# One TensorE tile shape throughout, and the last batch tile's top layers in pieces on two engines

## The chip, the cores and the metric

The kernel runs on one core of one Trainium2 chip. The metric is the device time of one execution in microseconds, the median of the runs. The kernel before takes 656.53 us (3 runs, 656.3 to 657.41).

## The reference

A recommendation tower for 1024 samples. 32 embedding tables give `e` (1024 x 32 x 16). A compressed interaction network of three layers of 64 maps follows, and then three dense layers:

```python
x0 = xk = e
for W in (W0, W1, W2):                      # (32,32,64), (32,64,64), (32,64,64)
    xk = relu(einsum('bmd,bhd,mhk->bkd', x0, xk, W))
    outs.append(sum(xk, axis=2))
z = concatenate(outs, axis=1)               # 1024 x 192
h = concatenate([z, dense_ctx], axis=1)     # 1024 x 208
h = maximum(h @ W_top1 + b_top1, 0)         # 512
h = maximum(h @ W_top2 + b_top2, 0)         # 256
y = h @ W_top3                              # 1
```

All of it is computed in float32.

## The kernel before, in words

The batch is cut into 8 tiles of 128 samples; a tile has two sides (A, Bs) of 64 samples, and a side two blocks of 32 samples, 512 columns (sample, d) each. Partitions hold pairs (m, h). The work is a list of 48 phases (tile, layer, side), lines 56 to 62, in which the layers of neighbouring tiles and sides are interleaved. In the steady part the order is (i, 2, A), (i+1, 0, A), (i, 2, Bs), (i+1, 0, Bs), (i+1, 1, A), (i+1, 1, Bs).

A phase is a list of steps. In each step VectorE (L692) or GpSimd (L401) multiplies the current maps by a copy of x0, 128 x 1024, into a ring (`z`, 6 places; `z_pool`, 4 places), and TensorE multiplies the product with 128 x 64 weights (L470), once per block: block 0 writes PSUM partitions 0 to 63 of the phase's accumulator, block 1 partitions 64 to 127. Two matmuls of 128 x 64 x 512, in two column groups of the array, are a step; the profile has each matmul as two records. Layers 1 and 2 have 16 steps, of which GpSimd makes 3 to 5 (line 66). Layer 0 has 4 steps, for the pairs of different embeddings, and one more product for the diagonal: ScalarE squares 32 rows (L521) and TensorE multiplies them by 32 x 64 weights (L466), from partitions 0 to 31 for side A and 32 to 63 for side Bs.

ScalarE fills the operand banks `xk` in PSUM (L535, L544, L553, L560), empties the accumulators (L571 for the next layer, L577 for the sums) and copies the sums of the layers, which VectorE reduces (L668), into the inputs of the top layers, `in12` and `in3` (L589). The top layers of tile i-1 are put into the step lists of tile i by hand (H1_AT, H2_AT, Y_AT, line 154): make_h1 (L417, L418) before step 12 of (i, 1, Bs), make_h2 (L425) before step 6 and make_y (L432) before step 13 of (i, 2, A). Each is a run of matmuls of 128 x 128 (80 x 128; 128 x 1 for y) on 128 streamed columns into one PSUM bank, `top`; ScalarE takes the results (L596, L603, L611).

GpSimd's queue carries, besides its products, the gathers of the embeddings of later tiles (L355). SP's queue stores gathered rows to DRAM (L275), loads them back as `lay`, `x0rep` and `squares` (L284, L296, L288) when their buffers are free, and, between the loads of side A and of side Bs, waits for y of tile i-2, loads the context rows (L340) and stores y (L341). ScalarE's queue loads the weights at the start.

After the last step the kernel runs 4 filler matmuls on 512 columns (L409), make_h1, 2 fillers, make_h2 and make_y for tile 7, each waiting for ScalarE's whole step before it (line 477 to 481, 649 to 654).

Of the kernel before, what the change touches and what calls it, by code (L numbers as in the profile page):

```python
# [15 lines left out]
H = 64  # L16
# [123 lines left out]
SUM_ROWS = [(layer, side) for layer in range(3) for side in range(SIDES)]  # L140
SUMS = {}
# [15 lines left out]
N_TOP_LOADS = 8  # L157


def build(nc, ids, ctx_t, tables, sel, ident, w0a, w0b, w0d, w1, w2, wt1, bt1, wt2, bt2, wt3, out):  # L160
    with ExitStack() as stack:
# [7 lines left out]
        w0d_sb = sb("w0d_sb", [SIDES * M, H])  # L169
# [13 lines left out]
        squares = sb("squares", [SIDES * M, WIDE])  # L183
# [11 lines left out]
        y_sb = sb("y_sb", [1, P])  # L195
# [32 lines left out]
        reduced = sem("reduced")  # L228
        inputs_in = sem("inputs_in")
        unit_ready = sem("unit_ready")  # L230
        unit_taken = sem("unit_taken")
        y_out = sem("y_out")

# [13 lines left out]
        def _(sp):  # L247
# [38 lines left out]
            def load_rows(i, side):  # L286

                sp.dma_start(squares[side * M:(side + 1) * M, :],  # L288
                             bass.AP(x0_rows, columns(i, side), [[PITCH, M], [1, WIDE]])).then_inc(rows_in[side], 16)
# [40 lines left out]
            for i in range(1, NT):  # L330
# [6 lines left out]
                if i > 1:  # L337
# [3 lines left out]
                    sp.dma_start(out[i - 2:i - 1, :], y_sb[:]).then_inc(y_out, 16)  # L341
# [5 lines left out]
            sp.dma_start(out[i - 2:i - 1, :], y_sb[:]).then_inc(y_out, 16)  # L347
            sp.wait_ge(unit_taken, 3 * (NT - 1) + 3)
            sp.dma_start(out[NT - 1:NT, :], y_sb[:]).then_inc(y_out, 16)
# [55 lines left out]
        def _(pe):  # L405
            def keep_busy(count, at):

                for _ in range(count):
                    pe.matmul(at[0:H, :], w1_sb[:, 0, :],  # L409
                              w1_sb[:, 0:COLS // H, :].rearrange("p t k -> p (t k)"), start=True, stop=True)  # L410

            def make_h1(i):
                pe.wait_ge(inputs_in, i + 1)
                pe.wait_ge(ctx_in, 16 * (i + 1))
                for m in range(F1 // P):
                    o = top[:, m * P:(m + 1) * P]
# [12 lines left out]
            def make_y(i):  # L429
                pe.wait_ge(unit_taken, 3 * i + 2)  # L430
                for k in range(F2 // P):
                    last = pe.matmul(top[0:1, 0:P], wt3_sb[:, k:k + 1], h2[:, k, :],  # L432
                                     start=(k == 0), stop=(k == F2 // P - 1))
                last.then_inc(unit_ready, 1)

# [7 lines left out]
            for n, (i, layer, side) in enumerate(PHASES):  # L443
# [5 lines left out]
                for k, (who, tile, _, _) in enumerate(STEPS[n]):  # L449
# [25 lines left out]


            keep_busy(4, xk[:, 0, 0:COLS])
            make_h1(NT - 1)
            keep_busy(2, xk[:, 0, 0:COLS])
            make_h2(NT - 1)  # L480
            make_y(NT - 1)

        @block.scalar
        def _(act):
# [18 lines left out]
            for side in range(SIDES):  # L503
                act.dma_start(w0d_sb[side * M:(side + 1) * M, :], w0d).then_inc(top_in, 16)
# [12 lines left out]
            def square(i, side):  # L517

                act.wait_ge(rows_in[side], 16 * (i + 1))
                of_side = squares[side * M:(side + 1) * M, :]  # L520
# [58 lines left out]
            def inputs(i, rows=range(len(SUM_ROWS))):  # L579
# [10 lines left out]
                if row == len(SUM_ROWS) - 1:  # L590
                    op.then_inc(inputs_in, 1)

# [14 lines left out]
            def take_y(i):  # L607
# [3 lines left out]
                act.activation(y_sb[:], top[0:1, 0:P], ACT.Copy).then_inc(unit_taken, 1)  # L611
# [38 lines left out]
            evacuate(taken)  # L650
            inputs(NT - 1, range(len(SUM_ROWS) - 1, len(SUM_ROWS)))
            take_h1(NT - 1)
# [96 lines left out]
```

## Time and profile before

| | us |
|---|---|
| median of 3 runs | 656.53 |
| the profiled execution, its own time | 655.24 |
| its span, first to last instruction | 653.3 |
| TensorE busy | 586.3 (90%) |
| VectorE busy | 545.9 (84%) |
| GpSimd busy | 513.9 (79%) |
| ScalarE busy | 353.2 (54%) |

TensorE's clock was granted in full (2.4 GHz) for 0.984 of the span; below it lie the start and a stretch after 222 us. Times in the rows are us from the span's start. Engines: PE is TensorE's matmuls, PEld its weight loads, DVE VectorE, ACT ScalarE, POOL GpSimd, SP the DMA-issuing engine. Matmuls are pipelined and the ends of their records are modelled, so the distance between starts tells their cost, not the duration.

### The profile page before, as it was taken

Reading aid. Unit: us, or ns where it says so; the run is one execution under the profiler, and the core shown is the slowest. Engines: PE = TensorE matmul, PEld = TensorE weight load, DVE = VectorE, ACT = ScalarE, POOL = GpSimd, SP = SyncE. Lnnn points to the kernel's source line nnn. Section 1 sums busy time; section 2 is a strip of 40 time slices with the busy share of each in tenths; the row PEclk is TensorE's granted clock in tenths of the full one; section 3 lists DMA queues with packets and bytes.
Section 4 is the critical chain, followed back from the end, with each engine's and each line's share of the span. In section 5 each row is a group of like instructions: output and inputs, shape, how many; then the busy total and the mean of one; then the engine's idle time right before and its main releaser. Section 6 shows DMA issues by size and latency. Waiting matters only on the chain.

```text
span 653.3 us, 7670 instructions
## 1 busy us (share of the span) xinstructions
PE 586.3 (90%) x2692; PEld 200.6 (31%) x2692; DVE 545.9 (84%) x345; ACT 353.2 (54%) x540; POOL 513.9 (79%) x373
## 2 busy tenths in 40 slices
PE   0027789899999799999999999999999999999998
PEld 0002223232333233332343324332333333333434
DVE  0002989899998799999999999999999998999780
ACT  0002574455756447555666666555755576666541
POOL 6777769388889888988898888888888876568650
PEclk9999799999999799999999999999999999999999
DMA  8649999950189917994499639990899249950000
GB/s 256 174 54 250 253 177 238 271 159 4 17 179 234 244 32 134 236 233 97 66 248 234 154 29 218 233 222 8 166 224 248 59 81 255 219 133 0 1 2 0
DMA packets 88438, 98.67 MB, mean 151 GB/s; under 512 B 59880, under 2 KB 66416, under 8 KB 88384
## 3 DMA queue, kind: packets, MB, share of 16 engines
q1 hardware_dynamic: 76064, 90.11, 60.4%
q0 software_dynamic: 8192, 2.11, 3.2%
q10 hardware_dynamic: 4144, 5.96, 2.8%
q8 instruction: 21, 0.34, 0.2%
q14 instruction: 17, 0.14, 0.1%
HBM read 95.01 MB, written 7.61 MB: 157 GB/s over the span
## 4 chain that ended last, share of the span: by engine, by line
PE 69%; DVE 6%; DMA 5%; ACT 5%; issue 2%; DVEq 0%; ACTq 0%
PE acc L470 61%; DVE z L692 6%; DMA x0rep<-x_rows 5%; ACT xk L560 3%; PE top L425 2%; PE acc L466 2%; PE top L417 1%; PE top L418 1%; PE xk L409 1%; ACT xk_copy L571 1%; PE top L432 1%; ACT xk L535 0%; ACT squares L521 0%; ACT xk L553 0%; DVEq L688 0%
## 5 line engine op out<-in xcount | busy, mean ns | idle before, releaser
L692 DVE TENSOR_TENSOR z<-xk,x0rep 128x2048 f32<-128x2048 f32 (+1 forms) x295 | 520.1, 1821 | 55.2 <-DMA x0rep<-x_rows 26.9
L470 PE MATMUL acc<-z,w_sb 128*64 128x512 f32 x1852 | 439.6, 605 | 20.3 <-DVE z L692 20.0
L401 POOL TENSOR_TENSOR z_pool<-x0rep,xk_copy 128x1024 f32<-128x1024 f32 x113 | 268.6, 2379 | 49.6 <-PE acc L470 32.2
L355 POOL DMA_INDIRECT emb<-tbl,idx x256 | 245.1, 957 | 68.6 <-issue 62.4
L470 PEld LDWEIGHTS acc<-z,w_sb 128*64 128x64 f32 x1852 | 128.4, 138 | 298.9 <-issue 225.3
L560 ACT ACTIVATE xk<-xk_copy 32x1024 f32<-32x1024 f32 x128 | 130.5, 1019 | 102.7 <-DVE z L692 101.4
L470 PE MATMUL acc<-z_pool,w_sb 128*64 128x512 f32 x452 | 116.4, 593 | 0.0
L571 ACT ACTIVATE xk_copy<-acc 64x512 f32<-64x512 f32 x128 | 75.5, 590 | 8.7 <-PE acc L470 7.6
L553 ACT ACTIVATE xk<-lay 128x1024 f32<-128x1024 f32 x16 | 16.4, 1028 | 78.3 <-DVE z L692 62.4
L409 PE MATMUL acc<-w_sb 128*64 128x512 f32 x24 | 12.4, 665 | 44.1 <-DMA emb<-tbl,idx 44.1
L470 PEld LDWEIGHTS acc<-z_pool,w_sb 128*64 128x64 f32 x452 | 32.1, 137 | 63.1 <-issue 60.8
L668 DVE TENSOR_REDUCE row_sums<-layer_out 128x32 f32<-128x512 f32 x48 | 32.3, 674 | 5.9 <-ACT layer_out L577 5.9
L535 ACT ACTIVATE xk<-xk_copy 128x1024 f32<-128x1024 f32 x31 | 31.7, 1022 | 7.8 <-DVE z L692 7.4
L577 ACT ACTIVATE layer_out<-acc 128x512 f32<-128x512 f32 x48 | 28.5, 594 | 8.5 <-PE acc L470 7.6
L535 ACT ACTIVATE xk<-lay 128x1024 f32<-128x1024 f32 x16 | 16.4, 1028 | 27.2 <-DMA lay<-x_rows 25.1
L660 DVE TENSOR_TENSOR w_sb<-w_sb,z 128x256 f32<-128x256 f32 x1 | 0.4, 424 | 34.5 <-DMA w_sb<-w0a_twice 34.5
L589 ACT ACTIVATE in<-row_sums 64x32 f32<-64x32 f32 x96 | 21.8, 227 | 6.7 <-DVE row_sums L668 5.7
L409 PEld LDWEIGHTS acc<-w_sb 128*64 128x64 f32 x24 | 3.6, 154 | 51.7 <-issue 51.7
L521 ACT ACTIVATE squares<-squares 32x1024 f32<-32x1024 f32 x16 | 16.8, 1050 | 4.5 <-DMA squares<-x_rows 4.3
L466 PE MATMUL acc<-squares,w0d_sb 32*64 32x512 f32 x64 | 18.1, 642 | 0.1
L425 PEld LDWEIGHTS top<-h,wt_sb 128*128 128x128 f32 x128 | 14.9, 191 | 6.5 <-issue 5.7
L535 ACT ACT_TABLE_LOAD x1 | 1.3, 1283 | 28.1 <-issue 28.1
(19 smaller groups left out, 97.6 us busy)
## 6 DMA issues: line engine op xcount, KB each, us to landing
x0rep<-x_rows SPq DMA_DIRECT2D x128, 512.0 KB, 16.0
lay<-x_rows SPq DMA_DIRECT2D x32, 512.0 KB, 9.9
emb<-tbl,idx POOLq DMA_INDIRECT x256, 2.4
w_long<-w ACTq DMA_DIRECT2D x4, 768.0 KB, 6.9
squares<-x_rows SPq DMA_DIRECT2D x16, 128.0 KB
x_rows<-emb SPq DMA_DIRECT2D x7, 256.0 KB, 4.6
x_rows<-emb SPq DMA_DIRECT2D x9, 128.0 KB, 6.1
w_sb<-w_long ACTq DMA_DIRECT2D x8, 128.0 KB
```

The source lines that it names most:

```text
L355: pool.indirect_dma_start(out=emb[:, i % 2, m, :], out_offset=None, in_=tables[m], in_offset=bass.IndirectOffsetOnAxis(ap=idx[:, i, m:m + ...
L401: pool.tensor_mul(z_pool[:, (count - 1) % POOL_RING, :], x0rep[:, g % X0_GROUPS, slot, :], xk_copy[:, side, :]).then_inc(z_pool_ready, 1)
L409: pe.matmul(at[0:H, :], w1_sb[:, 0, :], w1_sb[:, 0:COLS // H, :].rearrange("p t k -> p (t k)"), start=True, stop=True)
L425: last = pe.matmul(top[:, m * P:(m + 1) * P], wt2_sb[:, k, m * P:(m + 1) * P], h1[:, k, :], start=(k == 0), stop=(k == F1 // P - 1))
L466: pe.matmul(bank[c * H:(c + 1) * H, :], w0d_sb[side * M:(side + 1) * M, :], squares[side * M:(side + 1) * M, c * COLS:(c + 1) * COLS], sta ...
L470: mm = pe.matmul(bank[c * H:(c + 1) * H, :], w[:, tile, :], src[:, c * COLS:(c + 1) * COLS], start=(k == 0), stop=last)
L535: act.activation(xk[:, 0, :], src, ACT.Copy).then_inc(xk_ready[0], 1)
L560: op = act.activation(xk[q * Q:(q + 1) * Q, 1, :], xk_copy[other * Q:(other + 1) * Q, side, :], ACT.Copy)
L571: op = act.activation(xk_copy[half * H:(half + 1) * H, side, c * COLS:(c + 1) * COLS], bank[c * H:(c + 1) * H, :], ACT.Relu)
L577: act.activation(layer_out[:, n % OUTS, :], bank, ACT.Relu).then_inc(acc_taken, 1)
L668: dve.tensor_reduce(row_sums[:, i % 2, SUM_ROWS.index((layer, side)), :], layer_out[:, n % OUTS, :].rearrange("p (b d) -> p b d", d=D), AX ...
L692: dve.tensor_mul(z[:, at:at + wide, :], both, src).then_inc(z_ready, wide)
```

## The change

- The diagonal's weights and squares take 128 partitions. Rows 32 to 127 are set to zero once by VectorE at the start, and both sides use rows 0 to 31. The first loads into them wait for that (`cleared`).
- Every 128-column weight tile of make_h1 and make_h2 becomes two of 64 columns, one for each half of the PSUM partitions. make_y swaps its operands: `h2` is loaded as weights, 64 columns at a time, and the one column of `wt3` is streamed; y comes out as 128 partitions x 1 and is stored from there. Fillers run as pairs, one in each half.
- The last tile has its own path. The part of make_h1 that needs `in12` runs before the last sums are there, into free banks of `xk`, then one filler pair. The last accumulator is emptied in two halves (ScalarE) and reduced in two (VectorE); each of the two copies one block into `in3`. h1's four blocks and h2's two are taken in turn by ScalarE and VectorE, each as soon as it is made; make_h2's outer loop is over its inputs. y of this tile keeps the old form.

```diff
-        w0d_sb = sb("w0d_sb", [SIDES * M, H])
+        w0d_sb = sb("w0d_sb", [P, H])
-        squares = sb("squares", [SIDES * M, WIDE])
+        squares = sb("squares", [P, SIDES, WIDE])
-        y_sb = sb("y_sb", [1, P])
+        y_sb = sb("y_sb", [P, 1])
+        y_last = sb("y_last", [1, P])
...
+                if i == 0:
+                    sp.wait_ge(cleared, 1)
+                sp.dma_start(squares[0:M, side, :],
...
-                    sp.dma_start(out[i - 2:i - 1, :], y_sb[:]).then_inc(y_out, 16)
+                    sp.dma_start(out[i - 2:i - 1, :].rearrange("o p -> p o"), y_sb[:]).then_inc(y_out, 16)
...
+            halves = [slice(n * H, (n + 1) * H) for n in range(2)]
+
             def keep_busy(count, at):
-                for _ in range(count):
-                    pe.matmul(at[0:H, :], w1_sb[:, 0, :],
+                for n in range(2 * count):
+                    pe.matmul(at[halves[n % 2], :], w1_sb[:, 0, :],
                               w1_sb[:, 0:COLS // H, :].rearrange("p t k -> p (t k)"), start=True, stop=True)
+            def columns_of(m, half):
+                return slice(m * P + half * H, m * P + (half + 1) * H)

             def make_h1(i):
...
-                    o = top[:, m * P:(m + 1) * P]
-                    pe.matmul(o, wt1_sb[:, 0, m * P:(m + 1) * P], in12[:], start=True, stop=False)
-                    last = pe.matmul(o, wt1_sb[0:K3, 1, m * P:(m + 1) * P], in3[:], start=False, stop=True)
+                    for half in range(2):
+                        pe.matmul(top[halves[half], m * P:(m + 1) * P], wt1_sb[:, 0, columns_of(m, half)],
+                                  in12[:], start=True, stop=False)
+                    for half in range(2):
+                        last = pe.matmul(top[halves[half], m * P:(m + 1) * P], wt1_sb[0:K3, 1, columns_of(m, half)],
+                                         in3[:], start=False, stop=True)
...
             def make_h2(i):
...
-                        last = pe.matmul(top[:, m * P:(m + 1) * P], wt2_sb[:, k, m * P:(m + 1) * P],
-                                         h1[:, k, :], start=(k == 0), stop=(k == F1 // P - 1))
+                        for half in range(2):
+                            last = pe.matmul(top[halves[half], m * P:(m + 1) * P], wt2_sb[:, k, columns_of(m, half)],
+                                             h1[:, k, :], start=(k == 0), stop=(k == F1 // P - 1))
...
             def make_y(i):
...
-                    last = pe.matmul(top[0:1, 0:P], wt3_sb[:, k:k + 1], h2[:, k, :],
-                                     start=(k == 0), stop=(k == F2 // P - 1))
+                    for half in range(2):
+                        last = pe.matmul(top[halves[half], 0:1], h2[:, k, halves[half]], wt3_sb[:, k:k + 1],
+                                         start=(k == 0), stop=(k == F2 // P - 1))
...
+            def make_last():
+                h1_bank = [xk[:, m // 2, m % 2 * COLS:m % 2 * COLS + P] for m in range(F1 // P)]
+                h2_bank = [acc[:, (len(PHASES) + m) % ACCS, 0:P] for m in range(F2 // P)]
+                pe.wait_ge(last_in12, 1)
+                for m in range(F1 // P):
+                    for half in range(2):
+                        pe.matmul(h1_bank[m][halves[half], :], wt1_sb[:, 0, columns_of(m, half)], in12[:],
+                                  start=True, stop=False)
+                keep_busy(1, top)
+                pe.wait_ge(last_in3_act, 1)
+                pe.wait_ge(last_in3_dve, 1)
+                pe.wait_ge(ctx_in, 16 * NT)
+                for m in range(F1 // P):
+                    for half in range(2):
+                        op = pe.matmul(h1_bank[m][halves[half], :], wt1_sb[0:K3, 1, columns_of(m, half)], in3[:],
+                                       start=False, stop=True)
+                    op.then_inc(last_h1_made, 1)
+                pe.wait_ge(acc_taken, len(PHASES) - 1)
+                for k in range(F1 // P):
...
+                    for m in range(F2 // P):
+                        for half in range(2):
+                            op = pe.matmul(h2_bank[m][halves[half], :], wt2_sb[:, k, columns_of(m, half)], h1[:, k, :],
+                                           start=(k == 0), stop=(k == F1 // P - 1))
...
+                pe.wait_ge(last_h2_act, 1)
+                pe.matmul(top[0:1, 0:P], wt3_sb[:, 0:1], h2[:, 0, :], start=True, stop=False)
+                pe.wait_ge(last_h2_dve, 1)
+                pe.matmul(top[0:1, 0:P], wt3_sb[:, 1:2], h2[:, 1, :], start=False, stop=True).then_inc(last_y_made, 1)
...
-                            pe.matmul(bank[c * H:(c + 1) * H, :], w0d_sb[side * M:(side + 1) * M, :],
-                                      squares[side * M:(side + 1) * M, c * COLS:(c + 1) * COLS],
+                            pe.matmul(bank[c * H:(c + 1) * H, :], w0d_sb[:],
+                                      squares[:, side, c * COLS:(c + 1) * COLS],
...
-            keep_busy(4, xk[:, 0, 0:COLS])
-            make_h1(NT - 1)
-            keep_busy(2, xk[:, 0, 0:COLS])
-            make_h2(NT - 1)
-            make_y(NT - 1)
+            make_last()
...
-            for side in range(SIDES):
-                act.dma_start(w0d_sb[side * M:(side + 1) * M, :], w0d).then_inc(top_in, 16)
+            act.wait_ge(cleared, 1)
+            act.dma_start(w0d_sb[0:M, :], w0d).then_inc(top_in, 16)
...
+            for n in range(2):
+                cols = slice(n * COLS // 2, (n + 1) * COLS // 2)
+                act.activation(layer_out[:, taken % OUTS, cols], bank[:, cols], ACT.Relu).then_inc(last_out, 1)
...
+            dve.memset(w0d_sb[:], 0.0)
+            dve.memset(squares[:], 0.0).then_inc(cleared, 1)
```

## Rows read from the trace of the kernel before

**Rows 1.** The page's chain that ended last, by line
```profile
PE acc L470 61%; DVE z L692 6%; DMA x0rep<-x_rows 5%; ACT xk L560 3%; PE top L425 2%; PE acc L466 2%; PE top L417 1%; PE top L418 1%; PE xk L409 1%; ACT xk_copy L571 1%; PE top L432 1%; ACT xk L535 0%; ACT squares L521 0%; ACT xk L553 0%; DVEq L688 0%
```

**Rows 2.** Stretch: length, busy us of PE, PEld, DVE, ACT, POOL; PEclk, DMA share, GB/s
```profile
254.19:325.00 70.81, 69.98 (x335) 24.15 (x333) 69.60 (x44) 43.75 (x67) 62.41 (x47) 1.00 0.77 163
325.00:395.13 70.13, 69.67 (x334) 24.39 (x333) 68.80 (x45) 43.77 (x67) 62.04 (x46) 1.00 0.75 164
...
536.06:605.11 69.05, 69.05 (x333) 24.59 (x333) 64.46 (x44) 44.99 (x69) 45.98 (x20) 1.00 0.63 153
```

**Rows 3.** Waits (us, times, longest) of VectorE in 183:254, 254:325 and 325:395
```profile
DVE z L692 <- DMA x0rep<-x_rows: 5.8, 3, 3.2
...
DVE z L692 <- PE acc L470: 1.1, 2, 0.7
...
DVE z L692 <- PE acc L470: 1.3, 2, 1.1
```

**Rows 4.** Timeline of PE: start, us, what, records
```profile
224.67 1.97 PE L466 MATMUL acc<-squares,w0d_sb 32*64 32x512 f32 x4
...
254.12 0.49 PE L417 MATMUL top<-in,wt_sb 128*128 128x128 f32 x2
...
255.79 0.39 PE L418 MATMUL top<-in,wt_sb 80*128 80x128 f32 x2
256.11 1.08 PE L470 MATMUL acc<-z,w_sb 128*64 128x512 f32 x4
257.01 1.03 PE L470 MATMUL acc<-z_pool,w_sb 128*64 128x512 f32 x4
257.87 5.32 PE L470 MATMUL acc<-z,w_sb 128*64 128x512 f32 x24
...
264.84 2.05 PE L425 MATMUL top<-h,wt_sb 128*128 128x128 f32 x16
266.82 2.79 PE L470 MATMUL acc<-z,w_sb 128*64 128x512 f32 x12
...
272.98 0.60 PE L432 MATMUL top<-h,wt_sb 128*1 128x128 f32 x4
273.51 1.08 PE L470 MATMUL acc<-z_pool,w_sb 128*64 128x512 f32 x4
274.42 4.46 PE L470 MATMUL acc<-z,w_sb 128*64 128x512 f32 x20
278.81 1.07 PE L466 MATMUL acc<-squares,w0d_sb 32*64 32x512 f32 x4
279.81 3.65 PE L470 MATMUL acc<-z,w_sb 128*64 128x512 f32 x16
```

**Rows 5.** Weight loads by shape: count, busy us, mean ns of one, idle before
```profile
L470 PEld LDWEIGHTS acc<-z_pool,w_sb 128*64 128x64 f32 x452 | 32.1, 137 | 63.1 <-issue 60.8 <-POOL z_pool L401 2.3
...
L425 PEld LDWEIGHTS top<-h,wt_sb 128*128 128x128 f32 x128 | 14.9, 191 | 6.5 <-issue 5.7 <-ACT h L596 0.8
```

**Rows 6.** Timeline of the end, PE's weight loads left out
```profile
641.00 0.60 ACT L577 ACTIVATE layer_out<-acc 128x512 f32<-128x512 f32 x1 [5.88 <-PE acc L470]
641.63 0.69 DVE L668 TENSOR_REDUCE row_sums<-layer_out 128x32 f32<-128x512 f32 x1 [5.88 <-ACT layer_out L577]
642.41 0.47 ACT L589 ACTIVATE in<-row_sums 64x32 f32<-64x32 f32 x2 [0.81 <-DVE row_sums L668]
644.31 0.49 PE L417 MATMUL top<-in,wt_sb 128*128 128x128 f32 x2
...
646.40 1.14 ACT L596 ACTIVATE h<-top,bt_sb 128x128 f32<-128x128 f32 x4 [3.52 <-PE top L418]
648.16 2.05 PE L425 MATMUL top<-h,wt_sb 128*128 128x128 f32 x16
...
651.56 0.27 ACT L611 ACTIVATE y_sb<-top 1x128 f32<-1x128 f32 x1 [0.69 <-PE top L432]
```

**Rows 7.** All waits of VectorE: the one for the first weights
```profile
DVE w_sb L660 <- DMA w_sb<-w0a_twice: 34.5, 1, 34.5
```

More of the change, by code:

```diff
@@ L232, in build @@
         y_out = sem("y_out")
+        last_out = sem("last_out")
+        last_summed = sem("last_summed")
+        last_in12 = sem("last_in12")
+        last_in3_act = sem("last_in3_act")
+        last_in3_dve = sem("last_in3_dve")
+        last_h1_made = sem("last_h1_made")
+        last_h1_act = sem("last_h1_act")
+        last_h1_dve = sem("last_h1_dve")
+        last_h2_made = sem("last_h2_made")
+        last_h2_act = sem("last_h2_act")
+        last_h2_dve = sem("last_h2_dve")
+        last_y_made = sem("last_y_made")
+        last_y_taken = sem("last_y_taken")
         x0_rows = nc.dram_tensor("x0_rows", (X_ROWS, PITCH), F32)
@@ L519, in square @@
                 act.wait_ge(rows_in[side], 16 * (i + 1))
-                of_side = squares[side * M:(side + 1) * M, :]
+                of_side = squares[0:M, side, :]
                 act.activation(of_side, of_side, ACT.Square).then_inc(squares_ready, 1)
@@ L591, in inputs @@
                     op.then_inc(inputs_in, 1)
+                elif row == rows[-1]:
+                    op.then_inc(last_in12, 1)
             def take_h1(i):
@@ L649, in _ @@
             inputs(NT - 1, range(len(SUM_ROWS) - 1))
-            evacuate(taken)
-            inputs(NT - 1, range(len(SUM_ROWS) - 1, len(SUM_ROWS)))
-            take_h1(NT - 1)
-            take_h2(NT - 1)
-            take_y(NT - 1)
+            bank = acc[:, taken % ACCS, :]
+            act.wait_ge(step_done, STEP_ENDS[taken])
+            act.wait_ge(reduced, SUMMED.index(PHASES[taken - OUTS]) + 1)
+            for n in range(2):
+                cols = slice(n * COLS // 2, (n + 1) * COLS // 2)
+                act.activation(layer_out[:, taken % OUTS, cols], bank[:, cols], ACT.Relu).then_inc(last_out, 1)
+            act.wait_ge(last_summed, 2)
+            act.activation(in3[0:H, LAST_IN3:LAST_IN3 + ROWS], row_sums[0:H, (NT - 1) % 2, len(SUM_ROWS) - 1, :], ACT.Copy
+                           ).then_inc(last_in3_act, 1)
+            for m in range(0, F1 // P, 2):
+                act.wait_ge(last_h1_made, m + 1)
+                act.activation(h1[:, m, :], xk[:, m // 2, 0:P], ACT.Relu, bias=bt1_sb[:, m:m + 1]
+                               ).then_inc(last_h1_act, 1)
+            act.wait_ge(last_h2_made, 1)
+            act.activation(h2[:, 0, :], acc[:, len(PHASES) % ACCS, 0:P], ACT.Relu, bias=bt2_sb[:, 0:1]
+                           ).then_inc(last_h2_act, 1)
+            act.wait_ge(last_y_made, 1)
+            act.activation(y_last[:], top[0:1, 0:P], ACT.Copy).then_inc(last_y_taken, 1)
         @block.vector
@@ L694, in _ @@
                         sum_over_d(phase)
-            sum_over_d(PHASES[-1])
+            n = len(PHASES) - 1
+            sums = row_sums[:, (NT - 1) % 2, len(SUM_ROWS) - 1, :]
+            for half in range(2):
+                dve.wait_ge(last_out, half + 1)
+                rows = layer_out[:, n % OUTS, half * COLS // 2:(half + 1) * COLS // 2]
+                dve.tensor_reduce(sums[:, half * ROWS // 2:(half + 1) * ROWS // 2],
+                                  rows.rearrange("p (b d) -> p b d", d=D), AX_X, ALU.add).then_inc(last_summed, 1)
+            dve.wait_ge(last_summed, 2)
+            dve.tensor_copy(in3[0:H, LAST_IN3 + ROWS:LAST_IN3 + 2 * ROWS], sums[H:P, :]).then_inc(last_in3_dve, 1)
+            for m in range(1, F1 // P, 2):
+                dve.wait_ge(last_h1_made, m + 1)
+                dve.tensor_scalar(h1[:, m, :], xk[:, m // 2, COLS:COLS + P], bt1_sb[:, m:m + 1], 0.0, ALU.add, ALU.max
+                                  ).then_inc(last_h1_dve, 1)
+            dve.wait_ge(last_h2_made, 2)
+            dve.tensor_scalar(h2[:, 1, :], acc[:, (len(PHASES) + 1) % ACCS, 0:P], bt2_sb[:, 1:2], 0.0, ALU.add, ALU.max
+                              ).then_inc(last_h2_dve, 1)
 def kernel(**inputs):
```

19 lines of the change are left out of this document (13 added, 6 removed).

## The prediction

> **What bounds the kernel now.** I read the chain of waits first: L470, the layers' matmuls, holds 61% of it, and the top layers (L417 to L432) and the diagonal (L466) small parts [rows 1]. Then the table by stretches: the four middle batch tiles (254 to 536 us) take 70.8 and 70.1 us in turn (two of the four are shown), in which TensorE is busy 69.7 to 70.0 us and VectorE 68.8 to 69.6 us. Two engines are nearly full there. From 536 us on VectorE has over 4 us to spare and TensorE none [rows 2]. Then who waits for whom: in those two tiles VectorE waits for TensorE 1.1 and 1.3 us [rows 3]. So time taken from TensorE is worth at most 1.1 to 1.3 us per middle tile; after 536 us it is worth all of itself.
>
> **What a change of tile shape costs today.** A regular step is 4 records of 128x512 in two groups of 64 columns; inside a run it takes 0.86 us (257.01 to 257.87), or 0.2145 per record, while the first step after another shape takes 0.90 (256.11 to 257.01): 0.05 lost coming out. The 20 records from 274.42 should end 4.29 later, at 278.71; the diagonal starts at 278.81: 0.10 lost going in. The diagonal lasts 1.00 (to 279.81) for work of 0.86: 0.14 lost. Together 0.29 [rows 4]. The others, in the same rows, with 0.10 and 0.05 added at their ends:
> - H1 (L417, L418): 254.12 to 256.11, 1.99, so 2.14 us for 8 matmuls 128x128.
> - H2 (L425): 264.84 to 266.82, 1.98, so 2.13.
> - Y (L432): 272.98 to 273.51, 0.53, so 0.68.
>
> The Trainium skill has this as a rule (TensorEngine Tiling (Array Packing), Key Properties): changing the tiling mode, not only the tile, drains TensorE. The trace agrees, by the 0.29 us above.
>
> **Part 1, one shape, per tile.** *Diagonal*: 128 rows, 96 of them zero, should stream as long as 32 do, since the 512 columns stay; 0.29 saved twice a tile, 0.58. *H1, H2*: each 128-column matmul becomes a pair of 64-column ones. Two column groups run side by side in the trace: two of 512 columns in 0.86. So a pair of 128 streamed columns should take a quarter, 0.214, and 8 pairs 1.71: 0.43 and 0.42 saved. But no row issues such pairs; the records double from 16 to 32 in the same time. Bounds: 0.214 per pair if streaming binds; 0.48 if the halves don't overlap (7 matmuls of H1 take 255.79 - 254.12 = 1.67, 0.24 each, twice). Between lies 2 x 0.137 = 0.274, where each 64-column load [rows 5] must end before its own matmul may stream. I take 0.214: the 128-column loads last 191 ns [rows 5] and yet two are passed in each 0.24 us, so loads overlap matmuls. *Y*: its matmuls now stream one column each but load 64 columns 8 times. Bounds 8 x 0.137 = 1.10, all in a row, and 0.1; I take 0.45, loads in two groups side by side: 0.23 saved (-0.4 to +0.6). H1, H2 and Y together 1.08 per tile.
>
> The Trainium skill speaks against it (TensorE: Matmul & The Clock Gate, Back-to-back issue gap): about 81 ns per matmul in a sustained stream of loads and 128-column matmuls. By it a pair of four records costs 0.324 us and the whole would end near 657. No row here shows such a stream.
>
> **Where it counts.** (a) Start: the first diagonal stands in front of ScalarE's first fill (L544), which VectorE, and then GpSimd with the gathers that gate the next loads, follow: 0.3. What tile 0's top layers save near 190 us is lost in the waits for x0rep behind them (5.8 us [rows 3]). (b) At 222 to 254 us the chain is on TensorE, at the lower clock first (its diagonal takes 1.97 instead of 1.07 [rows 4]): 0.35. (c) Middle tiles: H1, H2 and Y lie ahead of VectorE's waits of 1.1 and 1.3, so 4 x 1.08 = 4.32. The diagonals lie behind them, where VectorE is full, and count for nothing. (d) From 536 us, all on TensorE: 2 x 1.08 + 0.58 = 2.74. Sum 7.7.
>
> **Part 2, the end.** Now [rows 6]: after the last step ScalarE runs from 641.00 to 641.60, VectorE to 642.32, ScalarE to 642.88. H1 starts at 644.31 only, behind four fillers (L409); h1 is taken from 646.40 to 647.54; H2 starts at 648.16, behind two more fillers; y is taken from 651.56 to 651.83. That is 10.83 us. New, an estimate from the same rows:
> - in12's half of H1 and one filler pair (4 x 0.214 + 0.86 = 1.7) fill 640.8 to 642.5 beside the sums.
> - Relu in two halves: 0.60 for 512 and 0.24 for 32 columns make 0.40 for 256; they end 641.40 and 641.70. Reductions of 0.42 (of 0.69): the second ends 642.24. Both halves of in3 by 642.53.
> - in3's part: block 0 ready 643.1, taken 643.5 (0.37 for one block, of 1.14 for four). Blocks alternate between ScalarE and VectorE, so the rest hides under H2.
> - H2: 643.56 + 8 x 0.22, last result 645.6; h2 645.9; Y's second half 646.35; y taken 646.65.
>
> From 641.00 that is 5.65: 5.2 saved (4.2 if each of VectorE's and ScalarE's pieces costs 0.15 more, 5.7 if they overlap better).
>
> **Costed at nothing.** The clearing memsets: VectorE then stands 34.5 us for a DMA [rows 7]; ScalarE's queue waits for them only after its long weight copies are issued, whose landing it needs next. Without that cover about 3 us. w0d's two loads become one. SP's squares loads: other partitions, same bytes. y leaves as 128 pieces on SP's queue ahead of side B's loads: no row prices it; up to 1 us is covered, since Y is that much sooner and side B with it. GpSimd is busy 62 of 71 us [rows 2], its queue full of gathers, but its products are read some us after they are made. The filler pairs stream side by side, in the time of one.
>
> **Sum.** The profiled execution took 655.24 us (span 653.3), 1.3 below the median of 656.53. Less 7.7 and 5.2: 642.3 against its own time, 643.6 against the median. I forecast **643.5**.
>
> **Rivals.**
> - *Paced pairs* (0.274 us): H1, H2 and Y save nothing. Left are 0.3 + 0.35 + 0.58 = 1.2 in the stream and 5.2 - 12 x 0.05 = 4.6 at the end: 5.8, **650.7**. For: doubled records. Against: loads overlap today.
> - *Slower: one after the other* (0.48). H1 and H2 cost 8 x 0.48 = 3.84, 1.75 more each, with Y 3.7 per tile, less 0.58. TensorE becomes the only bound: middle tiles need 69.8 + 3.1 = 72.9, 2.4 more each, 9.8; after 536 us 6.8; less 0.65 at the start and 5.2 - 12 x 0.26 = 2.1 at the end: +13.9, **670**. Its place is the load of the second half behind the first half's stream; it decides from about 0.32 per pair on. Against: pairs of 512 columns overlap.
> - *Cold end*: fewer fillers; if the clock falls to the lower level, 2.7 us of products double: **646**.
> - *Not the shape*: the 0.29 comes from the semaphore waits in front and stays. Only the end gains: **651.3**. For: each such place carries a wait. Against: four kinds lose the same 0.10 and 0.05.
>
> **How the numbers follow.** Forecast 0.60, paced pairs 0.20, pairs at the page's price 0.03, one after the other 0.08, cold end 0.05, not the shape 0.04. The range leaves out the two slow cases and runs from 640.5 (all bounds good) to 651.5 (paced pairs, and only the end). A measurement tells 0.2%, 1.3 us, from no change. Faster 0.89, same 0.03 (the page's price), slower 0.08.
>
> **What would show it.** Right: a diagonal follows L470 and is followed by it at 0.86 us; H1 takes about 1.75 us from its first matmul to the next L470; VectorE's waits for TensorE near 0 in the middle tiles, which take about 69.4; from the last L470 to y's copy about 5.7. Wrong: H1 over 2.1 us; middle tiles still above 70; new gaps in L470 for VectorE; a granted clock under 1 in the last 10 us.

## The result, and the profile after

| | before | after |
|---|---|---|
| median, us | 656.97 (4 runs, 656.3 to 658.43) | 648.5 (4 runs, 647.13 to 651.92) |
| profiled execution, its own time | 655.24 | 649.03 |
| its span | 653.3 | 647.2 |
| last step starts | 639.93 | 639.06 |
| from there to y taken | 11.90 | 6.66 |

The ratio is 0.9875 (95% interval 0.9846 to 0.9903): the kernel is faster by 1.25%, clear of the noise, and inside the range. The gain is 8.5 us where 13.0 were forecast, and the median lies 5.0 us above the 643.5. The two lower lines of the table say where: the end gave its 5.24 us (11.90 less 6.66), while the stream in front of it, which should have given 7.7, gave 0.87 (639.93 less 639.06).

First the shapes. The timeline of PE in the kernel after, the same stretch of the same tile as in [rows 4]; the columns are start, us, what, records:

```profile
255.96 0.39 PE L443 MATMUL top<-in,wt_sb 128*64 128x128 f32 x4
...
257.72 1.03 PE L538 MATMUL acc<-z,w_sb 128*64 128x512 f32 x4
...
266.30 1.92 PE L455 MATMUL top<-h,wt_sb 128*64 128x128 f32 x32
268.05 2.75 PE L538 MATMUL acc<-z,w_sb 128*64 128x512 f32 x12
...
274.06 0.35 PE L464 MATMUL top<-wt_sb,h 128*64 128x1 f32 x8
274.26 1.06 PE L538 MATMUL acc<-z_pool,w_sb 128*64 128x512 f32 x4
275.15 4.46 PE L538 MATMUL acc<-z,w_sb 128*64 128x512 f32 x20
279.44 1.03 PE L534 MATMUL acc<-squares,w0d_sb 128*64 128x512 f32 x4
280.30 3.17 PE L538 MATMUL acc<-z,w_sb 128*64 128x512 f32 x14
```

H1 takes 257.72 - 255.96 = 1.76 us (2.14 before), H2 268.05 - 266.30 = 1.75 (2.13), Y 0.20 (0.68), the diagonal 280.30 - 279.44 = 0.86 (1.00 before, 1.15 with what was lost in front of it and behind). The 20 records from 275.15 end 4.29 later, at 279.44, where the diagonal starts: no gap is left. All of this is as forecast, Y even cheaper.

The end, timeline of the kernel after without PE's weight loads, against [rows 6]:

```profile
639.06 1.03 PE L538 MATMUL acc<-z,w_sb 128*64 128x512 f32 x4
...
639.92 1.04 PE L475 MATMUL xk<-in,wt_sb 128*64 128x128 f32 x16
...
640.14 0.66 ACT L723 ACTIVATE layer_out<-acc 128x256 f32<-128x256 f32 x2 [5.88 <-PE acc L538]
640.56 0.75 DVE L784 TENSOR_REDUCE row_sums<-layer_out 128x16 f32<-128x256 f32 x2 [5.67 <-ACT layer_out L723]
...
640.80 1.03 PE L432 MATMUL top<-w_sb 128*64 128x512 f32 x4
641.34 0.23 ACT L725 ACTIVATE in<-row_sums 64x32 f32<-64x32 f32 x1 [0.54 <-DVE row_sums L784]
...
641.65 1.06 PE L483 MATMUL xk<-in,wt_sb 80*64 80x128 f32 x16
642.10 0.80 ACT L729 ACTIVATE h<-xk,bt_sb 128x128 f32<-128x128 f32 x2 [0.54 <-PE xk L483]
...
642.62 1.97 PE L495 MATMUL acc<-h,wt_sb 128*64 128x128 f32 x32
644.40 0.37 ACT L732 ACTIVATE h<-acc,bt_sb 128x128 f32<-128x128 f32 x1 [1.49 <-PE acc L495]
...
645.46 0.27 ACT L735 ACTIVATE y_last<-top 1x128 f32<-1x128 f32 x1 [0.69 <-PE top L502]
```

in12's half of H1 starts at 639.92 beside the sums, in3 is complete at 641.57, and h1 and h2 go in turns to ScalarE and VectorE. From the first relu (640.14) to y taken (645.73) are 5.59 us; before it was 10.83.

Then the stages. Stretches of the kernel after from one tile's H1 to the next (length, busy us of PE, PEld, DVE, ACT, POOL, then granted clock, DMA share, GB/s), against [rows 2]:

```profile
255.96:326.27 70.31, 69.00 (x370) 24.27 (x368) 69.48 (x44) 43.59 (x67) 61.90 (x47) 1.00 0.76 164
326.27:397.51 71.24, 69.29 (x370) 24.19 (x368) 68.71 (x45) 43.50 (x67) 62.58 (x46) 1.00 0.78 162
397.51:468.41 70.90, 69.23 (x371) 24.12 (x368) 69.48 (x44) 43.49 (x67) 61.91 (x46) 1.00 0.79 165
468.41:537.38 68.97, 68.45 (x371) 24.46 (x369) 68.61 (x45) 43.58 (x67) 60.38 (x42) 1.00 0.77 164
537.38:605.28 67.90, 67.47 (x370) 24.91 (x368) 63.20 (x42) 43.52 (x67) 45.94 (x20) 1.00 0.66 154
```

TensorE is busy 0.4 to 1.6 us less per stage, as it should be, but the second and third stages are as long as before or longer (71.24 against 70.13, 70.90 against 70.81), with neither engine full. What VectorE waited for in the four middle tiles (254 to 536 us), in the kernel after (us in total, times, longest):

```profile
DVE z L775 <- DMA x0rep<-x_rows: 4.4, 3, 2.2
DVE z L775 <- PE acc L538: 0.7, 2, 0.4
```

and the same question to the kernel before, which [rows 3] answered for two tiles:

```profile
DVE z L692 <- PE acc L470: 4.8, 8, 1.1
```

The waits for TensorE went, 4.8 to 0.7, which is about the gain that the forecast wanted (4.32). In their place stand 4.4 us for x0rep, a DMA, of which the kernel before had none there. The chain of the page tells the same (x0rep 5% in [rows 1]):

```profile
PE acc L538 49%; DMA x0rep<-x_rows 8%; DVE z L775 7%; ACT xk L624 6%; PE top L455 2%; PE acc L534 1%; PE top L446 1%; PE top L443 1%; PE acc L495 0%; SPq L302 0%; SPq L316 0%; ACT xk L599 0%; PE top L464 0%; PE xk L483 0%; PE xk L475 0%
```

And what SP issued just ahead of the late x0rep (timeline of SP, kernel after), with the wait of VectorE that followed (timeline of DVE):

```profile
345.36 0.42 SPq L361 DMA_DIRECT2D y<-y_sb  x1
345.81 0.43 SPq L308 DMA_DIRECT2D squares<-x_rows  x1
346.29 0.52 SPq L302 DMA_DIRECT2D lay<-x_rows  x1
```

```profile
366.40 3.49 DVE L775 TENSOR_TENSOR z<-xk,x0rep 128x1024 f32<-128x1024 f32 x3 [2.17 <-DMA x0rep<-x_rows]
```

The y store (L361) goes out 0.9 us before side B's first load, `lay` (L302). How long that load took from issue to landing (last column), in the kernel after and, in a second block, the same load of the kernel before:

```profile
lay<-x_rows SPq DMA_DIRECT2D x1, 512.0 KB, 11.2
```

```profile
lay<-x_rows SPq DMA_DIRECT2D x1, 512.0 KB, 5.5
```

This pair is the widest apart. The same load in five tiles, issued near 275, 345, 416, 487 and 557 us (us from issue to landing):

| | each tile | mean |
|---|---|---|
| before | 8.6, 5.5, 5.5, 5.3, 5.6 | 6.1 |
| after | 11.1, 11.2, 8.9, 8.6, 10.1 | 10.0 |

**Theory S:** the 128 pieces of 4 bytes in which y now leaves delay the loads behind them. **Rival F:** the doubled filler matmuls at the start cost the start 2.4 us (the fifth product is made at 68.98 against 66.59). **Rival V:** the stream's gain was never there, since VectorE is full in the middle tiles. **Rival W:** a faster TensorE brings VectorE to side B's loads too early, whatever the store is.

### The profile page after: what moved, and what is told of

Same layout as the page of the kernel before. It is cut to its first block, busy times and chain, and to the rows that moved or that the text cites. A ratio compares the mean times of both kernels' runs of the same rounds, so it can differ in the third digit from the quotient of the medians.

```text
span 647.2 us, 8272 instructions
## 1 busy us (share of the span) xinstructions
PE 574.6 (89%) x2992; PEld 200.6 (31%) x2992; DVE 548.0 (85%) x352; ACT 350.4 (54%) x537; POOL 513.5 (79%) x373
## 3 DMA queue, kind: packets, MB, share of 16 engines
q10 hardware_dynamic: 4096, 5.95, 2.9%
## 4 chain that ended last, share of the span: by engine, by line
PE 54%; DMA 8%; DVE 7%; ACT 6%; issue 2%; SPq 0%; DVEq 0%
PE acc L538 49%; DMA x0rep<-x_rows 8%; DVE z L775 7%; ACT xk L624 6%; PE top L455 2%; PE acc L534 1%; PE top L446 1%; PE top L443 1%; PE acc L495 0%; SPq L302 0%; SPq L316 0%; ACT xk L599 0%; PE top L464 0%; PE xk L483 0%; PE xk L475 0%
## 5 line engine op out<-in xcount | busy, mean ns | idle before, releaser
L534 PE MATMUL acc<-squares,w0d_sb 128*64 128x512 f32 x64 | 18.5, 659 | 0.2
L455 PEld LDWEIGHTS top<-h,wt_sb 128*64 128x64 f32 x224 | 12.7, 137 | 4.0 <-issue 4.0
## 6 DMA issues: line engine op xcount, KB each, us to landing
lay<-x_rows SPq DMA_DIRECT2D x32, 512.0 KB, 11.1
```

The costliest lines, as they stand in the source:

```text
L455: last = pe.matmul(top[halves[half], m * P:(m + 1) * P], wt2_sb[:, k, columns_of(m, half)], h1[:, k, :], start=(k == 0), stop=(k == F1 // ...
L534: pe.matmul(bank[c * H:(c + 1) * H, :], w0d_sb[:], squares[:, side, c * COLS:(c + 1) * COLS], start=False, stop=False)
```

## The experiments

Twelve kernels ran, in three launches; each is compared with the kernel before in its own launch (medians 655.97, 692.66 and 656.37 of 7, 12 and 17 runs; the others ran 4 to 10 times, "how long the pieces take" once). In the second launch the start of every kernel, the one before too, took about 36 us longer, so only differences are used from there.

### y as a row

From the kernel after; `wt3_sb` is 64 columns wider and zero there, so y is made by 64-column matmuls and leaves in one piece.

```diff
-                    for half in range(2):
-                        last = pe.matmul(top[halves[half], 0:1], h2[:, k, halves[half]], wt3_sb[:, k:k + 1],
+                    last = pe.matmul(top[0:H, 0:P], wt3_sb[:, k:k + H], h2[:, k, :],
...
-                    sp.dma_start(out[i - 2:i - 1, :].rearrange("o p -> p o"), y_sb[:]).then_inc(y_out, 16)
+                    sp.dma_start(out[i - 2:i - 1, :], y_sb[:]).then_inc(y_out, 16)
```

> The changed kernel, but y of tiles 0 to 6 is made as one row: wt3 as the first of 64 weight columns (the others zero or unused), h2 streamed, stored as one piece of 512 bytes. Shape 128*64 stays throughout. Theory S (the store in 128 pieces stalls SP's queue for some us just ahead of side B's loads; the changed kernel lost 0.81, 2.17, 1.39 and 1.31 us there): VectorE's waits for x0rep after 290 us vanish, middle tiles take about 69.4 us, the time is 5 to 6 us under the changed kernel's 648.5, near 643. Rival W (the faster TensorE brings VectorE to side B's loads too early, whatever the store is): the waits stay or grow, 648 to 649.

### y in the old form

From the kernel after: make_y and the store as they were, everything else new.

```diff
-                    for half in range(2):
-                        last = pe.matmul(top[halves[half], 0:1], h2[:, k, halves[half]], wt3_sb[:, k:k + 1],
+                    last = pe.matmul(top[0:1, 0:P], wt3_sb[:, k:k + 1], h2[:, k, :],
```

> The changed kernel with the old make_y (128x1 weights, one row, one piece). S: as the run with y as a row, but 7 changes of shape more at about 0.25 us each, of which those ahead of VectorE's waits count: 644 to 645. W: 648 to 650.

### The store behind the loads

From the kernel after: still 128 pieces, issued after side B's loads instead of ahead of them.

```diff
-                    sp.dma_start(out[i - 2:i - 1, :].rearrange("o p -> p o"), y_sb[:]).then_inc(y_out, 16)
                 load_side(i, Bs)
+                if i > 1:
+                    sp.dma_start(out[i - 2:i - 1, :].rearrange("o p -> p o"), y_sb[:]).then_inc(y_out, 16)
```

> The changed kernel, the 128-piece store of y kept but issued behind side B's loads instead of ahead of them. S: the stall falls behind the loads; waits for x0rep after 290 us vanish or fall under 1 us in all, 643 to 645. W: 648 to 649. If the stall hits what is already in flight, not what follows, side B's last loads suffer and the gain is between.

### The pieces alone

The kernel before with nothing but the new make_y and the 128-piece stores, the last y's too.

```diff
-            sp.dma_start(out[NT - 1:NT, :], y_sb[:]).then_inc(y_out, 16)
+            sp.dma_start(out[NT - 1:NT, :].rearrange("o p -> p o"), y_sb[:]).then_inc(y_out, 16)
```

> The kernel before, with only y's form and store changed as in the change (swapped operands, 128 x 1, 128 pieces; everything else old, at the pace of before). S: waits of VectorE for x0rep appear in middle tiles that had none, 2 to 5 us in all, time 657 to 661 beside 656.5. W: no new waits, 656 to 656.5, since TensorE is not faster but for 0.2 us per tile.

Measured, medians of one launch (before 655.97, 7 runs):

| | us | ratio (95%) |
|---|---|---|
| y as a row | 644.76 | 0.9823 (0.9802 to 0.9843) |
| y in the old form | 645.26 | 0.9843 (0.9819 to 0.9867) |
| store behind the loads | 644.78 | 0.983 (0.9814 to 0.9846) |
| the pieces alone | 670.54 | 1.021 (1.0188 to 1.0231) |

Any way to take the small writes from in front of the loads makes the gain about 11 us instead of 8.5 (10.7 to 11.2), and put alone into the kernel before they cost 14.6. The first three came out where S had them, within 2 us of it; the pieces alone cost far more than the 657 to 661 expected. The kernel after and "store behind the loads" differ in nothing but the place of the store (ratios 0.9875 and 0.983), so it isn't the pace of TensorE (W) that took the gain. The waits of VectorE in the same 282 us, with the store behind the loads:

```profile
DVE z L776 <- PE acc L539: 0.7, 2, 0.4
```

and with the pieces alone in the kernel before:

```profile
DVE z L695 <- DMA x0rep<-x_rows: 9.9, 6, 3.2
DVE z L695 <- PE acc L473: 3.5, 6, 1.1
```

Nothing for x0rep in the first, 9.9 us in the second; the kernel before had 0 there. The first load of side B, from issue to landing in the same five tiles (us):

| | each tile | mean |
|---|---|---|
| store behind the loads | 8.5, 7.2, 9.6, 9.4, 8.3 | 8.6 |
| y as a row | 9.3, 11.1, 6.9, 6.8, 7.2 | 8.3 |
| y in the old form | 8.0, 8.6, 7.9, 7.1, 5.1 | 7.3 |
| the pieces alone | 11.5, 10.3, 11.1, 8.6, 10.2 | 10.3 |

At the old pace the pieces make this load 4.2 us later (10.3 against 6.1); of the 3.9 us in the kernel after 1.4 to 2.7 are theirs, the rest came with the other fast kernels too. The last y adds its own part, which a timeline of SP shows:

```profile
662.61 0.36 SPq L349 DMA_DIRECT2D y<-y_sb  x1
```

The store is issued at 662.61 and the span ends at 670.5, 7.9 us later; in the kernel before these are 1.45 us (651.85 to 653.3). So 6.4 of the 14.6 are the last store, and about 8 the stages. In the profile the four middle tiles took 291.18 us against 281.87, 9.3 more. Part of that isn't the wait itself but the clock behind it (timeline of PE, pieces alone):

```profile
300.25 1.42 PE L473 MATMUL acc<-z,w_sb 128*64 128x512 f32 x4 [2.19 <-DVE z L695]
301.60 1.97 PE L469 MATMUL acc<-squares,w0d_sb 32*64 32x512 f32 x4
303.50 6.57 PE L473 MATMUL acc<-z,w_sb 128*64 128x512 f32 x20
```

VectorE had waited 3.23 us for x0rep, TensorE stood 2.19 us for VectorE, and then the granted clock was 0.65 of full from 300.25 to 310: the diagonal took 1.97 us instead of 1.07. The same came 146 us later, after 1.64 us of standing. Over these two tiles TensorE was busy 2.7 and 1.5 us more than in the kernel before. In the kernel after the clock stayed at 1.00 in all of these tiles.

One reservation: the first load can be slow without the pieces too. With y as a row it took 11.1 us at 343.7, an x0rep behind it landed near 363.7, and VectorE, which had waited 2.30 us, went on at 363.86; the trace puts this wait down to TensorE, but TensorE itself then ran out of products and stood 0.55 us until 365.14, so it wasn't behind. So the pieces make a late load frequent rather than being its only cause.

### How long the pieces take

The kernel before; behind its end five stores to a scratch tensor, each waited for: 128 pieces of 4 bytes at a pitch of 4, 64, 4096 and again 4 bytes, then one piece of 512 bytes. The output is complete; only the time is longer.

```diff
+            sp.dma_start(bass.AP(pieces, 0, [[1, P], [1, 1]]), bt1_sb[:, 0:1]).then_inc(pieces_out, 16)
+            sp.wait_ge(pieces_out, 16)
...
```

> The kernel before, and after its last store five stores to scratch memory, one after the other, each waited for: 128 pieces of 4 bytes at a pitch of 4 bytes (like y's), at 64 bytes, at 4096 bytes, at 4 bytes again, and one piece of 512 bytes. In the run with the 128-piece store at the end, that store took 7.9 us to the end of the span, one piece 1.45. Theory L (many small writes to the same 512 bytes queue up behind one another): 7 to 8 us at pitch 4, clearly less at 64 and about 2 at 4096. Theory N (a cost per piece, wherever it goes): 7 to 8 us at every pitch. One piece 1.5 to 2 in both. The time itself grows by the sum, 20 to 40 us.

```profile
689.04 0.36 SPq L353 DMA_DIRECT2D pieces<-bt_sb  x1
696.31 0.36 SPq L355 DMA_DIRECT2D pieces<-bt_sb  x1
697.74 0.32 SPq L357 DMA_DIRECT2D pieces<-bt_sb  x1
699.14 0.32 SPq L359 DMA_DIRECT2D pieces<-bt_sb  x1
706.80 0.24 SPq L361 DMA_DIRECT2D pieces<-y_sb  x1
```

Each is issued when the one before has landed: 7.27 us (pitch 4), 1.43 (64), 1.40 (4096), 7.66 (4 again), and 1.5 to the span's end for one piece. The number of pieces costs nothing here; that they lie side by side in 512 bytes costs 6 us, as if such writes queued up behind each other. (The run is one execution; pitch 4, run first and fourth, agrees within 0.4 us. It took 17.5 us more in all, where 20 to 40 were expected.) Where between 4 and 64 bytes the cost goes wasn't looked for, nor was a store of pieces 64 bytes apart put in front of the loads, so how the store holds up the loads behind it stays open. The Trainium skill (DMA: Bandwidth & Descriptors, its opening table) says that a transfer below 512 B is done as a read-modify-write. By that alone the pieces 64 B apart should suffer as well; they don't, so here the distance decides, not the size of a piece.

### The end alone

The kernel before with make_last and what belongs to it; the fillers in pairs, at the start too. The second version has the start's fillers in one half, as before.

```diff
-                for n in range(2 * count):
-                    pe.matmul(at[halves[n % 2], :], w1_sb[:, 0, :],
+                for n in range(2 * count if at is top else count):
+                    pe.matmul(at[halves[n % 2 if at is top else 0], :], w1_sb[:, 0, :],
```

> The kernel before with only the new end (last tile's top layers in pieces on two engines; the fillers run in pairs); all other tiles, diagonals and y as before. If the forecast's account of the end holds: from ScalarE's first relu to y's copy 5.65 us instead of 10.83, time 5.2 us under the kernel before, 650.8 beside 656.0. Rival (the end only looks short because the stream now ends elsewhere): under 3 us gained.

> The kernel before with the new end alone, now with the start as before the change. Theory: the first attempt lost 4 us at the start to the doubled instructions there, and the end is worth its 5.2 us whole: about 650.8 beside 656, the stretch from the last step's start to the end 6.7 us against 11.9, everything up to there within 0.5 us. Rival: the fillers were not the cause, and the start comes out later again than in its siblings.

First version 690.37 against 692.66, ratio 0.9962 (0.9947 to 0.9977); second 651.51 against 656.37, ratio 0.992 (0.9894 to 0.9946). Both have 6.66 us from the last step to y taken, and the stages of the second are 70.80, 70.46, 70.81, 70.12 and 69.06, those of before but for 0.33 in one. The second gives 4.9 of the 5.2 forecast (650.8 expected beside 656). The first gave 2.3 us, which by its number is the rival's "under 3"; its end was as short all the same. It lost 4 us at the start: its fifth product is at 108.06, those of its three siblings at 103.75 to 103.99. In that launch PE got an instruction only every 2.1 to 3.0 us there (timeline of PE, first version; the last column is the idle time before):

```profile
81.38 0.87 PE L430 MATMUL acc<-w_sb 128*64 128x512 f32 x1 [1.59 <-issue]
84.31 1.01 PE L430 MATMUL acc<-w_sb 128*64 128x512 f32 x1 [2.05 <-issue]
87.21 1.01 PE L430 MATMUL acc<-w_sb 128*64 128x512 f32 x1 [1.89 <-issue]
...
93.09 1.01 PE L531 MATMUL acc<-z,w_sb 128*64 128x512 f32 x1 [1.90 <-issue]
```

so the additional filler records there stood in line. That they cost the 4 us fits these rows; a version with single fillers wasn't run in that launch.

### The diagonal alone

The kernel before with w0d and squares on 128 partitions. It ran twice.

```diff
-                            pe.matmul(bank[c * H:(c + 1) * H, :], w0d_sb[side * M:(side + 1) * M, :],
+                            pe.matmul(bank[c * H:(c + 1) * H, :], w0d_sb[:],
```

> The kernel before with only the diagonal padded to 128 rows. Theory of two full engines: diagonals in the middle tiles lie where VectorE is full and are worth nothing; those at the start, at 225 us and the two after 536 us are: 0.3 + 0.2 + 0.58, about 1.1 us, 654.9. Rival (all 16 count on the path): 16 x 0.29 = 4.6 us, 651.4.

> The kernel before with the padded diagonal alone, again. Four tiles of two diagonals at 0.29 us each would be 2.3 us of TensorE time; theory: VectorE is full in these stages, so the middle tiles shorten by 0.1 to 0.2 us each and the last one by 0.6, 1.1 us in all: about 655 beside 656. Rival: the 3.7 us that its first measurement gave belong to the padding: 652.3.

688.95 against 692.66, ratio 0.9939 (0.9916 to 0.9961), and 653.97 against 656.37, ratio 0.9943 (0.9925 to 0.9961). The stages do what the theory says: in the first run's profile 70.62, 70.00, 70.61, 70.00 and 68.46 us against 70.81, 70.13, 70.81, 70.12 and 69.05, that is 0.1 to 0.2 each and 0.59 at the last, 1.2 in all, where 1.1 was expected. In the second run's profile they are 70.62, 70.86, 70.62, 69.99 and 68.46: one is longer than before. The medians give 3.7 and 2.4 (the second ratio 3.7), more than the stages account for. Between 1.2 and 3.7 the size stays open; a profiled execution of each is too few where the median itself moves by 1 us.

### The top layers in pairs

The kernel before with H1 and H2 in pairs and y as a row of 64 columns, the last tile's too; the order of the old end is kept.

```diff
-                    last = pe.matmul(top[0:1, 0:P], wt3_sb[:, k:k + 1], h2[:, k, :],
+                    last = pe.matmul(top[0:H, 0:P], wt3_sb[:, k:k + H], h2[:, k, :],
```

> The kernel before with only H1 and H2 in pairs of 64 columns and y as one row of a 64-column tile, stored in one piece; diagonal and end's order as before (the last tile's H1 and H2 in pairs too). Theory of two full engines: VectorE's 1.1 and 1.3 us of waiting go in each of four middle tiles, 4.3 us; after 536 us 2 x 1.1; the last tile's own H1 and H2 0.9; together 7 to 7.5 us, 648.7. Rival (the stream is bound elsewhere, in the loads of x0rep, and gives less): under 4 us.

687.29 against 692.66, ratio 0.9919 (0.989 to 0.9948): 5.4 us, less than the 7 to 7.5 expected and more than the rival's 4. With the end (4.9) and the diagonal (2.4 to 3.7) the parts make 12.7 to 14.0, the whole without small writes 11.2 to 11.5; what the last tile gains from pairs is in two of the parts.

Where it fell short is the middle tiles. The four stretches from H1 to H1 together, and what VectorE waited in them (us):

| kernel | four middle tiles | for TensorE | for x0rep |
|---|---|---|---|
| before | 281.87 | 4.8 | 0 |
| diagonal alone, two profiles | 281.23, 282.09 | 4.1, 4.8 | 0, 0.8 |
| top layers in pairs | 280.48 | 3.2 | 0.8 |
| kernel after, store behind the loads | 276.75 | 0.7 | 0 |

The pairs alone gave 1.4 us there instead of 4.3, the padded diagonal alone 0.6 at most, both together 5.1 (4.5 with y as a row and a late store). These are one profile each, and those of the second launch have no profile of the kernel before beside them; in "how long the pieces take", which up to its end is the kernel before, the same four take 282.14. With quicker top layers and the old diagonals VectorE waits for TensorE at a new place: 0.94 us at 469.26, behind the first diagonal of the tile that starts at 429.85; in the kernel before no wait stands there. So "the diagonals count for nothing" holds in these profiles only while the top layers are slow.

### The start, and the best version

From the kernel after, only the fillers at the start in one half again, the edit shown under "the end alone":

> The changed kernel with nothing but the matmuls that hold the clock at the start put back to one half (8 and 2 times 2 instead of twice as many). If the doubled instructions cost the start of the changed kernel the 2.4 us that its profile shows (fifth step's product at 68.98 against 66.59), this gives 646 to 647 beside the changed kernel's 648.5, and the fifth product at 66.5 to 67. If that was chance of one execution (the kernels with a row of y and the same doubled matmuls had it at 67.0 to 67.4), it gives 648 to 649.

And, with the same start, y as a row, its store behind the loads:

```diff
                 load_side(i, Bs)
+                if i > 1:
+                    sp.dma_start(out[i - 2:i - 1, :], y_sb[:]).then_inc(y_out, 16)
```

> The changed kernel with three edits: y as one row of 64-column matmuls that leaves in one piece, its store issued behind side B's loads, and matmuls that hold the clock at the start in one half of the columns as before the change. If the 128 small writes were the only loss, the row alone and the late store alone have each shown it already (about 11.2 us off the kernel before) and both together add nothing: 644 to 645 beside 656. If the place of the store behind the loads is worth something by itself (the late store reached 641.35 of span in its profile against 643.2 for the row), the two together give 642 to 643.

The first took 653.0 (7 runs, 651.16 to 653.74), ratio 0.9944 (0.9923 to 0.9965), the second 644.91, ratio 0.9829 (0.979 to 0.9867). Neither expectation of the first held (646 to 647, or 648 to 649): it is 4.5 us slower than the kernel after was in its launch. F falls: the fifth product is at 67.17 here, at 66.98 to 67.42 in three kernels with doubled fillers, at 68.36 in "the end alone" without them. What it goes with is the clock: from 62.5 to 67 us 0.62 and 0.61 of it were granted in the two late ones (68.98 in the kernel after, 68.36), 0.99 or 1.00 in the eight others with the usual start (66.59 to 67.42). VectorE's waits in 254 to 536 us show where this one lost its time:

```profile
DVE z L775 <- DMA x0rep<-x_rows: 7.3, 3, 2.8
DVE z L775 <- PE acc L538: 1.0, 3, 0.4
```

7.3 us for x0rep. The two kernels of this launch differ only in how y is made and stored, and by 8.1 us. So the price of the small writes is not one number: about 3 us for the kernel after (8.5 gained instead of 11.2), about 8 for the stages of "the pieces alone" and here. In the profiles it follows the waits for x0rep in the four middle tiles: 4.4 us, and 281.42 us against 277.38 for the version without small writes; 7.3 here, and 284.76; 9.9 in the pieces alone, and 9.3 more than before. Why the loads are later in one execution than in another isn't settled.

The stretches of the version without small writes, from H1 to H1:

```profile
255.14:324.76 69.62, 68.50 (x367) 33.96 (x365) 69.39 (x44) 43.62 (x67) 61.53 (x46) 1.00 0.75 165
324.76:393.76 69.00, 68.48 (x367) 33.83 (x365) 68.64 (x45) 43.63 (x67) 61.21 (x45) 1.00 0.73 164
...
532.52:599.82 67.30, 67.30 (x367) 39.94 (x364) 63.69 (x43) 44.07 (x68) 45.79 (x20) 1.00 0.64 160
```

69.62 us with VectorE busy 69.39, 69.00 with 68.64: VectorE is the bound there now, so V is true as a limit (a further cut on TensorE gives nothing in these tiles) but not as an objection. Row and late store together are worth no more than either alone, as expected (644 to 645), so some 644.8 us is the best that these versions give, 3.7 below the changed kernel's 648.5.

## Why the prediction was right, and where it failed

Its steps, from the profiles (us gained on the kernel before's profile, in its stretches from H1 to H1):

| step | forecast | kernel after | row, late store |
|---|---|---|---|
| (a), (b) up to the H1 at 254 us | 0.65 | -1.84 | -1.02 |
| (c) four middle tiles | 4.32 | 0.45 | 4.49 |
| (d) from 536 us to the last step | 2.74 | 2.26 | 2.65 |
| the end | 5.2 | 5.24 | 5.08 |
| sum | 12.9 | 6.1 | 11.2 |

- **The range held in part by luck.** Its upper end, 651.5, was set by paced pairs and by "only the end gains", neither of which came; the loss that did come had no place in it. One of the prediction's own signs of being wrong came true as well: three of the four middle tiles stayed above 70 us (70.31, 71.24 and 70.90).
- **The step that failed** stood under what was costed at nothing: "y leaves as 128 pieces on SP's queue ahead of side B's loads: no row prices it; up to 1 us is covered". It cost 4.4 us of new waits for x0rep in the middle tiles; the store's own landing, 6 us longer (7.3 to 7.7 against 1.4 us), isn't waited for there. The table shows it in (c): 0.45 instead of 4.32, and 4.49 once the pieces are away. The cover of 1 us was counted as if only side B's start moved; what moved were the landings of the loads (issued at 346.29 against 345.78 in the kernel before, landed 11.2 and 5.5 us later). Since no row priced it, its upper bound should have been in the range and in a rival of its own.
- **(c) was right in its sum and wrong in its parts.** It gave the 4.32 to H1, H2 and Y and nothing to the diagonals. The pairs alone, with the old diagonals, gave 1.4 us, and only both together 4.5 to 5.1 (table under "the top layers in pairs").
- **(a) and (b)** gained nothing, except 0.40 us in the profile of y as a row, whose H1 is at 253.72. In the version without small writes the loss lies in the waits for x0rep from 183 to 254 us (9.0 us against 5.8 in [rows 3]): they take up what TensorE gives, as was said of tile 0's top layers, and here also what was counted for the diagonal. In the kernel after it lies before its first H1, at 178.58 against 176.68, and goes with the clock: 0.62 of full between 62.5 and 67 us, the diagonal there 1.98 us long; in the four kernels of the first launch it was 0.99 or 1.00.
- **Pairs at streaming rate** (0.214 taken, rivals 0.274 and 0.48): 1.76 / 8 = 0.22. Right. The records doubled and each pair of 128-column matmuls costs a quarter of one of 512, so "paced pairs" and "one after the other" fall. The Trainium skill's figure (TensorE: Matmul & The Clock Gate, Back-to-back issue gap), 81 ns per matmul at 128 columns, would have made 0.324; the trace has 0.055 per record, four to a pair.
- **The gap of a changed shape**, 0.29 for the diagonal: gone, to 0.00. "Not the shape" falls. The Trainium skill (TensorEngine Tiling (Array Packing), Key Properties) has it that a change of the tiling mode drains TensorE; this trace agrees, with 0.29 us lost where the shape changed and 0.00 where it no longer does.
- **Y**: 0.45 taken, 0.20 measured, for eight records with eight loads of 64 columns, 0.025 us each, where a load by itself lasts 0.137.
- **The end**: 5.65 forecast, 5.59 measured, each hand-over within 0.1 to 0.3. No cold end: the granted clock is 1.00 from 640 to 646 us.
- **VectorE full in the middle**: its waits for TensorE fell from 4.8 to 0.7, and once the pieces were out of the way stages of 69.0 to 69.6 were reached, "about 69.4".

## What to carry to other kernels

Price a store by how its pieces lie in DRAM, not by its bytes: a result that comes out one element per partition is cheap to compute (0.20 us) and dear to store as neighbouring 4-byte pieces, and the dear part falls on the loads queued behind it. Keep such a result as a row, or issue its store behind the loads that matter. And once the only two busy engines are both full, a new small delay on the queue that feeds them counts in full (7.3 us of waits made the stages 7.4 us longer here), so look there first when a gain stays away. Where two engines are nearly even, don't add up what each change gives alone: a part that counts for nothing today can be the next bound.

## What the runs showed of the hardware that was not expected

- 128 writes of 4 bytes into the same 512 bytes take 7.3 to 7.7 us to land; the same number 64 or 4096 bytes apart take 1.4, as one write of 512 bytes does (1.5).
- A late load can cost twice: after TensorE had stood 2.19 us for it, the granted clock was 0.65 over the next 9.75 us, and a diagonal took 1.97 us instead of 1.07.
- A matmul in one half of the columns runs beside the other half's next step. y as a row of 64 columns, timeline of PE in that kernel:

```profile
270.53 1.46 PE L537 MATMUL acc<-z,w_sb 128*64 128x512 f32 x6
271.82 0.49 PE L463 MATMUL top<-h,wt_sb 128*64 128x128 f32 x3
272.04 0.64 PE L537 MATMUL acc<-z_pool,w_sb 128*64 128x512 f32 x1
...
272.95 2.47 PE L537 MATMUL acc<-z,w_sb 128*64 128x512 f32 x10
```

  Y's records and those of the next step (L537) lie among each other. Ten records of L537 would take 2.15 us from 270.53 on; the eleventh starts 2.42 us later, so Y costs 0.27 where the old form took 0.68.
- In one launch PE received an instruction only every 2.1 to 3.0 us for some 25 us of the start, which is part of the 36 us by which every kernel was longer there; what held it back wasn't found out.
